# A fused transformer, state-space and routed-expert block on one core: another order of the steps on all five queues, and other PSUM banks

## The chip, the cores and the metric

The kernel runs on one core of one Trainium2 chip. Times are device microseconds (us) of one launch. PE is TensorE, DVE VectorE, ACT ScalarE, POOL GpSimd and SP SyncE, whose queue only issues DMA transfers. The number to predict is the median time of the changed kernel.

## The reference

```
mod = (silu(c) @ wmod).reshape(32, 6, 1, 256)        # sa, ca, ga, sb, cb, gb
h = layernorm(x) * (1 + ca) + sa                      # x: 32 x 512 x 256
# inside block(h):
xn = ln1(h)
attn_out = softmax(causal(q k^T / 4)) v @ o_w + o_b   # 16 heads of 16
x_ssm, z = split(xn @ in_proj_w)                      # 512 channels each
x_c = silu(causal_conv4(x_ssm));  dt = softplus((x_c @ x_proj_w)[:R] @ dt_w + dt_b)
h_t = exp(dt A) h_(t-1) + x_c dt B_t ;  y_t = C_t h_t  # 16 states, 512 tokens
ssm_out = ((y + x_c D) * silu(z)) @ ssm_out_w
x1 = h + alpha attn_out + (1 - alpha) ssm_out
block = x1 + gelu(ln2(x1) @ ffn_w1 + b1) @ ffn_w2 + b2
x = x + ga * block(h)
h = layernorm(x) * (1 + cb) + sb
out = x + gb * (h @ base_w + b + 2 * sum_e softmax(top2(router)) lora_e(h))
```

## The kernel before

The 32 batches are worked off one after the other, in one unrolled stream. All weights stay in SBUF. Each engine has a queue of named steps, and the queue of a batch ("a turn") is a text in the table ORDER: a name with + is that step of the next batch, with - of the batch before, so that about three batches are in work at once. `drive` goes through the text once a batch. The order is thus written out as data. Each step waits for semaphores of the steps that feed it and then issues its instructions; nothing is reordered at run time. A second table, PLACE, gives each step that uses a PSUM bank one of four banks `pM`.

The state-space part is the backbone. It has 64 scans a batch (e = 0 to 63, two of them to a unit k = e/2), each over 128 channels and 512 tokens:

- ACT `decE` writes exp(dt A) to one of two banks `pD`, chosen by e mod 2 (L714).
- POOL `fillK` writes the two inputs of unit k to the ring `state` (L575). It needs the B row of unit k, which SP loads with `rbK` (L430), and room in the ring, which PE's `add` of scan 2k-7 gives.
- DVE `scanE` does the scan (L1207), and `cE` multiplies it by the C row (L1215; SP loads that row with `rcK`). For a quarter of the scans POOL does the multiplication (`pcE`, L563). Until `cE` (or, for those, `scanE`) has read bank `pD`, `dec(E+2)` can't start.
- PE `addE` transposes the product and adds it to `pY` (L945). `gate1` on DVE (L1282) takes the sums when all 64 are in, and PE `skip0` (L936) starts the next sums.

Around it, on the same queues: attention in four head groups (PE `mxG_E` scores, L1033 and L1035, whose maximum DVE takes, L1256; `mtG` turns the maxima and SP sends them back as a matrix row; PE `stG_*` scores again, L1051, ACT exponentials, L813; PE `pvG_*`, L967; DVE `onG` normalises, L1271 and L1273), projections, `sso` (L1073, L1076), the feed-forward part `f1_0` to `f1_7` (L1087), `gelu` (L854), `f2_0` and `f2_1` (PE L1096, DVE L1298), and routing.

ACT `sp2` is the softplus of dt: two instructions on 128 x 1024 elements (L795), with a table load ahead of them and another ahead of the next exponential. The change is in the tables alone; these functions of the kernel are as they were, for instance:

```
elif name == "sp2":
    for jp in range(PASSES):
        dt = dts[:, parity(b), jp * JP:(jp + 1) * JP]
        b.wait(act, dt_x, (jp + 1) * JP)
        act.activation(dt, dt, ACT.Softplus).then_inc(dt_ok.sem, 1)
```

Of the kernel before, what the change touches and what calls it, by code (L numbers as in the profile page):

```python
# [1351 lines left out]

ORDER = {engine: parse(text) for engine, text in {
    "SP": """
        -rc21 -ld3 -rb24 -rc24 -rc23 -rc25 -rb26 -mt2 -rb25 qk3 -rb27 -rc26 -rb29 -rc28 xp -rc27 -rb30 -rb28 -mt3
        ld0 -rb31 rb0 -rc29 -rc30 rc0 l1a rb3 ld2 -rc31 rc1 rc2 rb1 rb4 rb2 rc3 rb5 +load rc4 rb8 rc5 rb6 ld1 -xr
        rc6 rb7 rc8 rc9 rc7 rb9 rb11 rb12 rb13 rc10 rb10 rc11 rc14 rc13 mt0 rc12 rb16 rc15 rb14 rc17 rb15 rc16 rb17
        rb18 rc18 rb19 +qk0 +qk1 +qk2 rc20 rb20 mt1 rc19 x1p rb21 rb22 rc22 rb23 -put
    """,
    "POOL": """  # L1360
        fill7 fill8 +l0s fill9 pc14 pc15 +l0a fill10 +l0b fill11 +l0c fill12 pc22 +l1s fill13 pc23 -x2 -x2b fill14
        -l3s +ql0 fill15 fill16 pc30 -xb +ql1 -route -wkeep fill17 -wnorm pc31 +ql2 fill18 fill19 -gb -put fill20
# [4 lines left out]
        dec5 dec6 z0 dec7 dec8 dec9 dec10 dec11 z1 -l2a dec12 z2 -h2t0 -h2t1 dec13 dec14 dec15 -f1_0 -f1_1 -f1_2
        dec16 -f1_3 dec17 +l0a dec18 -f1_4 -f1_5 dec19 dec20 -f1_6 -f1_7 -gelu dec21 mt0 dec22 z3 dec23 dec24 dec25
        zsilu dec26 +l1a dec27 +xt0 +xt1 st0_0_0 +qk0 dec28 st0_0_1 +qm0 st0_0_2 dec29 +xs0 st0_0_3 st0_1_0 -l3a
        st0_1_1 +qk1 dec30 +qm1 dec31 -h3t0 +xs1 -h3t1 dec32 +qk2 dec33 -route2 st0_1_2 st0_1_3 dec34 mt1 +qm2 -axt  # L1370
        +qk3 dec35 dec36 st0_2_0 -out0 st0_2_2 dec37 -out1 dec38 st0_3_0 st1_0_0 dec39 st1_0_1 st1_0_2 dec40 oe0
        st1_0_3 st1_1_0 st1_1_1 dec41 st1_1_2 st1_1_3 st1_2_0 dec42 dec43 +qm3 st1_2_2 +xs2 +xs3 st1_3_0 dec44 mt2
        dec45 +xsilu dec46 oe1 dec47 +xp st2_0_0 st2_0_1 dec48 st2_0_2 dec49 +dt0 st2_0_3 st2_1_0 dec50 st2_1_1
        dec51 st2_1_2 +dt1 st2_1_3 dec52 mt3 +dt2 st2_2_0 dec53 st2_2_2 dec54 st2_3_0 st3_0_0 st3_0_1 dec55 st3_0_2
        dec56 st3_0_3 dec57 +dt3 oe2 st3_1_0 dec58 dec59 +sp2 dec60 st3_1_1 st3_1_2 st3_1_3 dec61 st3_2_0 st3_2_2
# [3 lines left out]
        mx1_0 mx1_1 add17 add18 add19 -f2_0 -f2_1 mx1_2 +xt0 +xt1 mx1_3 add20 st0_0_0 mx1_4 mx1_5 +qk0 mx1_6 add21
        st0_0_1 +xs0 mx1_7 st0_0_2 mx1_8 add22 st0_0_3 st0_1_0 add23 add24 add25 add26 st0_1_1 +qk1 -h3t0 add27  # L1380
        -h3t1 +xs1 +qk2 -route add28 mx1_9 mx1_10 st0_1_2 add29 st0_1_3 -lora mt1 +qk3 add30 -axt st0_2_0 pv0_0
        -out0 st0_2_2 add31 mx2_0 -out1 mx2_1 st0_3_0 pv0_1 mx2_2 pv0_2 skip1 st1_0_0 pv0_3 mx2_3 mx2_4 add32 add33
        st1_0_1 mx2_5 st1_0_2 mx2_6 add34 mx2_7 mx2_8 st1_0_3 st1_1_0 st1_1_1 mx2_9 pv1_0 add35 st1_1_2 st1_1_3
        add36 st1_2_0 mx2_10 st1_2_2 st1_3_0 +xs2 pv1_1 add37 +xs3 add38 add39 add40 mt2 add41 add42 add43 pv1_2
        mx3_0 mx3_1 pv1_3 on0 mx3_2 +xp mx3_3 mx3_4 add44 st2_0_0 st2_0_1 add45 st2_0_2 mx3_5 +dt0 mx3_6 mx3_7
        st2_0_3 add46 st2_1_0 add47 st2_1_1 mx3_8 st2_1_2 mx3_9 +dt1 st2_1_3 mx3_10 add48 +dt2 mt3 pv2_0 add49
        st2_2_0 st2_2_2 add50 add51 st2_3_0 pv2_1 pv2_2 st3_0_0 st3_0_1 +dt3 st3_0_2 add52 st3_0_3 pv2_3 st3_1_0
        add53 on1 +mx0_0 on2 st3_1_1 add54 +mx0_1 add55 add56 +mx0_2 +v0 add57 +mx0_3 st3_1_2 st3_1_3 add58 pv3_0
        st3_2_0 st3_2_2 pv3_1 st3_3_0 pv3_2 add59 pv3_3 +z0 +v1 on3 add60 add61 +mx0_4 add62 add63 ot0 ot1 +skip0
        yt0 yt1 yt2 +add0 yt3 +add1 +add2 sso0 sso1 +add3 +z1 +add4 +mx0_5 +z2 +add5 +add6 +add7 +add8 +mx0_6 +add9  # L1390
        h2t0 h2t1 +mx0_7 +add10 +add11 +mx0_8 f1_0 f1_1 f1_2 f1_3 f1_4 +mx0_9 f1_5 f1_6 f1_7 +add12 +add13 +add14
        +mx0_10 +add15 +z3 +mt0 +add16
    """,
    "DVE": """
        c13 +l0s scan14 scan15 scan16 c16 scan17 c17 scan18 c18 scan19 mx0_9 c19 mx0_10 scan20 mx1_0 c20 mx1_1
        scan21 c21 scan22 mt0 scan23 +l1s -f2_0 scan24 c24 scan25 c25 scan26 c26 -f2_1 mx1_2 mx1_3 scan27 mx1_4
# [1 line left out]
        mx1_10 c32 +qk2 -esum scan33 -lora mt1 scan34 c33 c34 +qk3 scan35 scan36 c35 mx2_0 c36 gate0 scan37 mx2_1
        scan38 mx2_2 c37 mx2_3 mx2_4 scan39 mx2_5 mx2_6 mx2_7 mx2_8 scan40 mx2_9 scan41 c40 c41 mx2_10 scan42 scan43
        c42 c43 +xs2 +xs3 mt2 scan44 mx3_0 mx3_1 c44 scan45 on0 mx3_2 c45 scan46 mx3_3 scan47 mx3_4 mx3_5 scan48  # L1400
        scan49 mx3_6 mx3_7 c48 c49 mx3_8 scan50 mx3_9 c50 mx3_10 scan51 mt3 c51 scan52 c52 scan53 c53 scan54 scan55
# [55 lines left out]
```

## Time and profile before

| | |
|---|---|
| three runs | 5529.20, 5524.32, 5529.31 us; median 5529.2 |
| the profiled execution | 5525.26 us, span 5523.5 us |
| PE busy | 5113.2 us (93%) |
| DVE busy | 4999.6 us (91%) |
| POOL busy | 4215.9 us (76%) |
| ACT busy | 3967.2 us (72%) |
| mean DMA rate | 147 GB/s |

Busy time is the union of an engine's instructions. In steady state every engine's queue repeats each turn, so one turn can be read for all. PE's ends are modelled, so a full PE is read from its starts: in a stretch where it has no gap, it is the bound.

### The profile page before, as it was taken

What the parts mean: (1) busy time and instruction counts of PE and PEld (TensorE: products, weight loads), DVE (VectorE), ACT (ScalarE), POOL (GpSimd) and SP (SyncE); (2) the same over time, 40 slices, a digit from 0 to 9 for tenths busy, and PEclk for the clock granted to TensorE, in tenths of its full rate; (3) what the DMA queues carried; (4) which work ended last, traced back from release to release, by engine and by line L of the source; (5) the groups of instructions that cost most, each with busy time, mean ns of one, the idle gap of its engine ahead of it and who ended that gap; (6) DMA issues with size and microseconds to landing.
All of it is one profiled execution on the core that took longest, in us unless ns stands there. A gap on an engine that the chain in (4) does not pass through costs nothing.

```text
span 5523.5 us, 94525 instructions
## 1 busy us (share of the span) xinstructions
PE 5113.2 (93%) x32280; PEld 3450.1 (62%) x32280; DVE 4999.6 (91%) x7745; ACT 3967.2 (72%) x6278; POOL 4215.9 (76%) x2641
## 2 busy tenths in 40 slices
...
GB/s 127 140 145 149 153 161 153 146 148 147 155 161 152 142 151 148 156 161 152 142 148 151 154 163 149 143 148 148 153 166 149 142 148 147 155 167 147 144 141 28
DMA packets 521455, 812.22 MB, mean 147 GB/s; under 512 B 80432, under 2 KB 227288, under 8 KB 520976
## 3 DMA queue, kind: packets, MB, share of 16 engines
...
## 4 chain that ended last, share of the span: by engine, by line
PE 44%; DVE 32%; issue 12%; ACT 5%; DMA 3%; POOL 1%; SPq 1%; ACTq 1%; DVEq 0%; POOLq 0%
DVE pD L1207 10%; DVE mx L1256 7%; PE pY L945 7%; PE pM L967 5%; DVE state L1207 4%; PE pM L1076 4%; DVE state L1215 4%; PE pM L1020 3%; DMA bc<-bc_d 3%; PE pM L1051 3%; DVE xc L1247 3%; PE pM L954 2%; PE pM L1002 2%; PE pM L1073 2%; PE pM L1125 2%
## 5 line engine op out<-in xcount | busy, mean ns | idle before, releaser
L575 POOL TENSOR_TENSOR state<-scan_in,bc 128x1024 f32<-128x1024 f32 x1024 | 2412.0, 2365 | 687.1 <-PE pY L945 439.6
L1207 DVE TENSOR_TENSOR_SCAN pD<-pD,state 128x512 f32<-128x512 f32 x1536 | 1849.0, 1217 | 76.3 <-POOL state L575 38.1
L714 ACT ACTIVATE pD<-scan_in,A 128x512 f32<-128x512 f32 x2048 | 1393.6, 688 | 584.0 <-DVE state L1215 482.3
L945 PE MATMUL pY<-ident,state 128*128 128x128 f32 x8192 | 1142.1, 276 | 12.1 <-POOL state L563 7.7
L945 PEld LDWEIGHTS pY<-ident,state 128*128 128x128 f32 x8192 | 912.1, 142 | 260.1 <-issue 172.5
L1215 DVE TENSOR_TENSOR state<-pD,bc 128x512 f32<-128x512 f32 x1536 | 1024.4, 681 | 42.1 <-DMA bc<-bc_d 27.7
L813 ACT ACTIVATE region<-pM 128x512 f32<-128x512 f32 (+1 forms) x1408 | 754.7, 555 | 327.9 <-PE pM L1053 292.5
L1256 DVE TENSOR_REDUCE mx<-pM 128x1 f32<-128x512 f32 (+3 forms) x1408 | 859.7, 630 | 130.0 <-PE pM L1035 127.8
L563 POOL TENSOR_TENSOR state<-state,bc 128x512 f32<-128x512 f32 x512 | 645.5, 1273 | 268.7 <-DVE state L1207 263.5
L1207 DVE TENSOR_TENSOR_SCAN state<-pD,state 128x512 f32<-128x512 f32 x512 | 611.5, 1210 | 78.2 <-ACT pD L714 78.2
L1033 PE MATMUL pM<-region 96*128 96x512 bf16 (+3 forms) x2048 | 527.9, 303 | 120.8 <-DVE mx L1256 73.6
L1051 PE MATMUL pM<-region 98*128 98x512 bf16 (+3 forms) x2048 | 533.1, 302 | 75.0 <-DVE mx L1256 40.4
L1087 PE MATMUL pM<-region,w_f 128*128 128x512 f32 x1024 | 455.3, 598 | 0.9 <-ACT region L845 0.9
L1096 PE MATMUL pM<-w_f,scan_in 128*128 128x256 f32 x2048 | 449.0, 380 | 5.7 <-ACT scan_in L854 5.7
L1096 PEld LDWEIGHTS pM<-w_f,scan_in 128*128 128x128 f32 x2048 | 387.7, 191 | 58.5 <-ACT scan_in L854 6.5
L1033 PEld LDWEIGHTS pM<-region 96*128 96x128 bf16 x2048 | 199.8, 98 | 314.1 <-issue 106.8
L1035 PE MATMUL pM<-mask_qk,identb 128*128 128x128 bf16 x2048 | 394.8, 220 | 0.0
L1053 PE MATMUL pM<-identb,mask_qk 128*128 128x128 bf16 x2048 | 392.2, 220 | 0.0
L967 PE MATMUL pM<-region,vt 128*17 128x512 f32 (+3 forms) x4096 | 369.0, 438 | 0.6 <-ACT region L813 0.6
L1051 PEld LDWEIGHTS pM<-region 98*128 98x128 bf16 x2048 | 199.1, 98 | 266.0 <-ACT region L813 124.0
L1087 PEld LDWEIGHTS pM<-region,w_f 128*128 128x128 f32 x1024 | 190.4, 191 | 218.2 <-issue 208.7
L1247 DVE SCALAR_TENSOR_TENSOR xc<-pM,conv_w,xc 128x511 f32<-128x511 f32 (+2 forms) x384 | 285.6, 744 | 22.1 <-ACT xc L774 13.1
...
## 6 DMA issues: line engine op xcount, KB each, us to landing
...
region<-qk_d SPq DMA_DIRECT2D x256, 64.0 KB, 2.7
...
```

The lines of the kernel that those rows point to most:

```text
L563: nc.gpsimd.tensor_tensor(slot, slot, bc[:, e // JP % BC_SLOTS, 1, :], ALU.mult).then_inc(pp_ok.sem, 1)
L575: nc.gpsimd.tensor_tensor(state[:, at_:at_ + JP], us[:, parity(b), k // N * JP:(k // N + 1) * JP, :], bc[:, k % BC_SLOTS, 0, :].unsqueeze( ...
L714: act.activation(pD[DECAY_BANK[e]][:], dts[:, parity(b), j], ACT.Exp, scale=A[:, j, n:n + 1]).then_inc(a_ok.sem, 1)
L813: act.activation(probs[kb % 2][:, h:h + heads, 0:n], pM[bank_of(name)][:, 0:heads * n].rearrange("p (h t) -> p h t", h=heads), ACT.Exp, sc ...
L945: ins = pe.matmul(y_part(t, e % JP), state[:, e % RING, t * P:(t + 1) * P], ident[:], is_transpose=True, start=False, stop=(e % PASS >= PA ...
L1033: pe.matmul(ps[:, s * n:(s + 1) * n], q[0:QK_ROWS, h, qb * P:(qb + 1) * P], kk[0:QK_ROWS, h, 0:n], start=True, stop=False, skip_group_chec ...
L1051: pe.matmul(ps[:, i * n:(i + 1) * n], kk[0:QK_ROWS + 2, h + i, kb * P:(kb + 1) * P], q[0:QK_ROWS + 2, h + i, kb * P:L], start=True, stop=F ...
L1087: ins = pe.matmul(ps[:], w_f1[:, k, f * P:(f + 1) * P], h2T[:, k], start=(k == 0), stop=(k == KT - 1))
L1096: ins = pe.matmul(ps[:, t * D:(t + 1) * D], gT(b)[:, f, (2 * n + t) * P:(2 * n + t + 1) * P], w_f2[:, f, :], start=(f == 0), stop=(f == FT ...
L1207: v.tensor_tensor_scan(h if e in POOL_C else decay, decay, h, 0.0, ALU.mult, ALU.add)\
L1215: v.tensor_tensor(state[:, e % RING], pD[DECAY_BANK[e]][:], bc[:, slot, 1, :], ALU.mult)\
L1256: v.tensor_reduce(mx[:, g % 2].rearrange("p (h q) -> p h q", q=TB)[:, heads[0]:heads[-1] + 1, qb], pM[bank_of(name)][:, 0:len(heads) * n]. ...
```

## The change

The four texts of ORDER on the compute engines and that of SP are replaced, and the table PLACE with them. Every turn has the same steps with the same instructions as before. The diff of the tables says little to a reader; one pair of lines of it, from DVE's text:

```diff
-        scan56 scan57 c56 c57 on1 scan58 +mx0_0 on2 +mx0_1 scan59 +mx0_2 c58 +mx0_3 c59 scan60 c60 scan61
...
+        scan56 +mx0_0 c56 scan57 +mx0_1 c57 scan58 on2 c58 scan59 +mx0_2 c59 scan60 scan61 c60 c61 +mx0_3 scan62
```

The first place is PE's queue just ahead of the long step `f2_0`, `f2_1` (L1096). Before:

```order
L1020 MATMUL pM<-w_in,xnT 128x512 x2
L1041 MATMUL pM<-ident,mx 16x128
L945 MATMUL pY<-ident,state 128x128 x4
L1033 MATMUL pM<-region 128x512
L1035 MATMUL pM<-mask_qk,identb 128x128
L1033 MATMUL pM<-region 128x512
L1035 MATMUL pM<-mask_qk,identb 128x128
L945 MATMUL pY<-ident,state 128x128 x12
L1096 MATMUL pM<-w_f,scan_in 128x256 x32
```

After:

```order
L1020 MATMUL pM<-w_in,xnT 128x512 x2
L945 MATMUL pY<-ident,state 128x128 x4
L1041 MATMUL pM<-ident,mx 16x128
L1033 MATMUL pM<-region 128x512
L1035 MATMUL pM<-mask_qk,identb 128x128
L1033 MATMUL pM<-region 128x512
L1035 MATMUL pM<-mask_qk,identb 128x128
L945 MATMUL pY<-ident,state 128x128 x12
L1033 MATMUL pM<-region 128x512
L1035 MATMUL pM<-mask_qk,identb 128x128
L1096 MATMUL pM<-w_f,scan_in 128x256 x32
```

Two more `add` steps (of 4 matmuls each; the second one stands further up, behind `f1_7`) and one more `mx` step (`mx1_2`) now stand ahead of `f2_0`; they stood behind `f2_1` or later.

The second place is DVE's queue from the sum of `f2_0` to that of `f2_1` (both L1298). Before:

```order
L1298 TENSOR_TENSOR x<-x,pM 128x512
L1207 SCALAR_TENSOR_TENSOR pD<-pD,state 128x512
L1215 TENSOR_TENSOR state<-pD,bc 128x512
L1207 SCALAR_TENSOR_TENSOR pD<-pD,state 128x512
L1215 TENSOR_TENSOR state<-pD,bc 128x512
L1207 SCALAR_TENSOR_TENSOR pD<-pD,state 128x512
L1215 TENSOR_TENSOR state<-pD,bc 128x512
L1298 TENSOR_TENSOR x<-x,pM 128x512
L1256 TENSOR_REDUCE mx<-pM 128x1 x2
```

After:

```order
L1298 TENSOR_TENSOR x<-x,pM 128x512
L1215 TENSOR_TENSOR state<-pD,bc 128x512
L1207 SCALAR_TENSOR_TENSOR pD<-pD,state 128x512 x2
L1215 TENSOR_TENSOR state<-pD,bc 128x512 x2
L1298 TENSOR_TENSOR x<-x,pM 128x512
L1256 TENSOR_REDUCE mx<-pM 128x1
```

Before, the scans (L1207) between the two sums are 24, 25 and 26; now they are 26 and 27. So `scan27` and `c27`, which stood behind the sum of `f2_1`, stand ahead of it, and one of the two maxima behind it (`mx1_2`) has gone further up. At the start of the same stretch, `c0` and the maximum of `mx0_4` went from behind `gate1` to ahead of it, and `scan1` from ahead to behind.

The third place is DVE's queue beside ACT's softplus. Before, from `scan56` and `scan57` to `c58`:

```order
L1207 SCALAR_TENSOR_TENSOR pD<-pD,state 128x512 x2
L1215 TENSOR_TENSOR state<-pD,bc 128x512 x2
L1271 RECIPROCAL rden<-pM 128x16
L1273 TENSOR_TENSOR region<-pM,rden 128x4x64
L1207 SCALAR_TENSOR_TENSOR pD<-pD,state 128x512
L1256 TENSOR_REDUCE mx<-pM 128x1
L1271 RECIPROCAL rden<-pM 128x16
L1273 TENSOR_TENSOR region<-pM,rden 128x4x64
L1256 TENSOR_REDUCE mx<-pM 128x1
L1207 SCALAR_TENSOR_TENSOR pD<-pD,state 128x512
L1256 TENSOR_REDUCE mx<-pM 128x1
L1215 TENSOR_TENSOR state<-pD,bc 128x512
```

After:

```order
L1256 TENSOR_REDUCE mx<-pM 128x1
L1215 TENSOR_TENSOR state<-pD,bc 128x512
L1207 SCALAR_TENSOR_TENSOR pD<-pD,state 128x512
L1271 RECIPROCAL rden<-pM 128x16
L1273 TENSOR_TENSOR region<-pM,rden 128x4x64
L1215 TENSOR_TENSOR state<-pD,bc 128x512
L1207 SCALAR_TENSOR_TENSOR pD<-pD,state 128x512
L1256 TENSOR_REDUCE mx<-pM 128x1
L1215 TENSOR_TENSOR state<-pD,bc 128x512
L1207 SCALAR_TENSOR_TENSOR pD<-pD,state 128x512 x2
L1215 TENSOR_TENSOR state<-pD,bc 128x512 x2
```

The rows after are `mx0_1 c57 scan58 on2 c58 scan59 mx0_2 c59 scan60 scan61 c60 c61`. Between `c57` and `scan60` there stood `on1`, `scan58`, `mx0_0`, `on2`, `mx0_1`, `scan59`, `mx0_2`, `c58`, `mx0_3` and `c59`. Now `scan58`, `on2`, `c58`, `scan59`, `mx0_2` and `c59` stand there. On ACT `sp2` still stands between `dec59` and `dec60`; the exponential step `st3_1_1` went from behind it to ahead of it. On SP, `rb26` stood ahead of `xp` (the stores of the B and C rows of the next batch, L454 and L456) and now stands behind it.

## Rows read from the trace of the kernel before

**Rows 1.** The page: span, busy time, and the chain that ended last.

```profile
span 5523.5 us, 94525 instructions
PE 5113.2 (93%) x32280; PEld 3450.1 (62%) x32280; DVE 4999.6 (91%) x7745; ACT 3967.2 (72%) x6278; POOL 4215.9 (76%) x2641
PE 44%; DVE 32%; issue 12%; ACT 5%; DMA 3%; POOL 1%; SPq 1%; ACTq 1%; DVEq 0%; POOLq 0%
```

**Rows 2.** Gelu's instruction on ACT: its kind, and first and last start.

```profile
L854 ACT ACTIVATE scan_in<-scan_in x32: 3617/3620/3622, 325.5 to 5464.3; 128x4096 f32<-128x4096 f32 x32
```

**Rows 3.** Busy us and instructions by stretch: PE, PEld, DVE, ACT, POOL; PEclk, DMA, GB/s.

```profile
2708.80:2874.80 166.00, 157.97 (x1011) 106.92 (x1010) 155.75 (x243) 123.72 (x196) 131.60 (x83) 1.00 0.49 151
...
2775.60:2833.80 58.20, 58.19 (x296) 43.62 (x297) 53.48 (x85) 43.98 (x64) 48.44 (x34) 1.00 0.46 139
2833.80:2941.60 107.80, 99.77 (x715) 63.30 (x714) 102.26 (x158) 79.81 (x134) 83.17 (x49) 1.00 0.50 158
```

**Rows 4.** Who PE waited for in 2775.6 to 2833.8: us, times, longest.

```profile
PE pY L936 <- DVE zs L1282: 0.5, 1, 0.5
```

**Rows 5.** Who DVE waited for in 2833.8 to 2941.6, the two largest.

```profile
DVE state L1207 <- ACT pD L714: 2.4, 3, 0.9
DVE mx L1256 <- PE pM L1035: 2.0, 4, 0.7
```

**Rows 6.** Timeline of PE ahead of and in `f2`: start, us, instruction.

```profile
2818.35 0.38 PE L1033 MATMUL pM<-region 96*128 96x512 bf16 x1
...
2818.63 1.48 PE L945 MATMUL pY<-ident,state 128*128 128x128 f32 x12
2819.94 13.98 PE L1096 MATMUL pM<-w_f,scan_in 128*128 128x256 f32 x64
2833.76 0.38 PE L1033 MATMUL pM<-region 96*128 96x512 bf16 x1
```

**Rows 7.** Timeline of DVE beside the softplus, `c56` to `c60`.

```profile
2754.05 1.27 DVE L1215 TENSOR_TENSOR state<-pD,bc 128x512 f32<-128x512 f32 x2
...
2757.57 0.25 DVE L1271 RECIPROCAL rden<-pM 128x16 f32<-128x16 f32 x1
...
2758.20 0.68 DVE L1256 TENSOR_REDUCE mx<-pM 128x1 f32<-128x512 f32 x1
2758.79 1.22 DVE L1207 TENSOR_TENSOR_SCAN pD<-pD,state 128x512 f32<-128x512 f32 x1
2759.93 0.67 DVE L1256 TENSOR_REDUCE mx<-pM 128x1 f32<-128x512 f32 x1
2760.51 0.68 DVE L1215 TENSOR_TENSOR state<-pD,bc 128x512 f32<-128x512 f32 x1
2761.91 0.69 DVE L1256 TENSOR_REDUCE mx<-pM 128x1 f32<-128x512 f32 x1 [0.73 <-PE pM L1035]
2762.52 0.68 DVE L1215 TENSOR_TENSOR state<-pD,bc 128x512 f32<-128x512 f32 x1
2763.12 1.22 DVE L1207 TENSOR_TENSOR_SCAN pD<-pD,state 128x512 f32<-128x512 f32 x1
2764.38 0.69 DVE L1215 TENSOR_TENSOR state<-pD,bc 128x512 f32<-128x512 f32 x1
```

**Rows 8.** Timeline of ACT, `dec58` and `dec59`, the softplus and its two table loads.

```profile
2754.76 1.30 ACT L714 ACTIVATE pD<-scan_in,A 128x512 f32<-128x512 f32 x2 [0.16 <-DVE state L1215]
2756.08 1.28 ACT L795 ACT_TABLE_LOAD   x1
2757.38 2.00 ACT L795 ACTIVATE scan_in<-scan_in 128x1024 f32<-128x1024 f32 x2
2759.40 1.28 ACT L714 ACT_TABLE_LOAD   x1
```

**Rows 9.** Timeline of POOL: `fill28` and `fill29`.

```profile
2746.81 4.68 POOL L575 TENSOR_TENSOR state<-scan_in,bc 128x1024 f32<-128x1024 f32 x2 [5.87 <-DMA bc<-bc_d]
```

**Rows 10.** Timeline of SP: the second store of `xp`, and the row loads behind it.

```profile
2740.72 0.41 SPq L456 DMA_DIRECT2D bc_d<-dbc  x1
2741.17 1.45 SPq L430 DMA_DIRECT2D bc<-bc_d  x3
```

More of the change, by code:

```diff
@@ L1354 @@
     "SP": """
[L1355 to L1358, printed above, removed]
+        -rb24 -rb23 qk2 qk3 +load -ld3 -rc23 -rc25 -rb27 -mt2 -rb25 -rc24 -rc26 xp -rb28 -rb26 -rc27 -rb29 ld0 -rc28
@@ L1365 @@
+        fill31 +u0 +u1 +fill0 pc62 pc63 +fill1 +fill2 +fill3 +fill4 +pc6 +pc7 +fill5 l2s +fill6 +fill7
     """,
     "ACT": """
[L1367 to L1375, printed above, removed]
@@ new lines @@
+        dec36 +qk3 st0_1_3 dec37 -out0 -out1 dec38 st0_2_0 dec39 st0_2_2 st0_3_0 oe0 dec40 +qm3 dec41 st1_0_0
+        st1_0_1 st1_0_2 st1_0_3 st1_1_0 st1_1_1 st1_1_2 st1_1_3 dec42 st1_2_0 st1_2_2 dec43 +xs2 dec44 dec45 +xs3
+        st1_3_0 mt2 +xsilu oe1 dec46 dec47 +xp dec48 st2_0_0 dec49 st2_0_1 st2_0_2 +dt0 st2_0_3 st2_1_0 dec50 dec51
+        st2_1_1 st2_1_2 st2_1_3 st2_2_0 dec52 mt3 st2_2_2 dec53 dec54 +dt1 st2_3_0 dec55 +dt2 dec56 oe2 st3_0_0
+        dec57 st3_0_1 +dt3 st3_0_2 dec58 st3_0_3 st3_1_0 st3_1_1 dec59 +sp2 dec60 st3_1_2 st3_1_3 dec61 st3_2_0
@@ L1377 @@
+        st3_2_2 st3_3_0 dec62 oe3 dec63 +v0 +dec0 +ud +dec1 ot0 ot1 +v1 +dec2 yt0 +dec3 yt1 yt2 yt3 +dec4
     """,
     "PE": """
[L1379 to L1392, printed above, removed]
+        add18 mt0 mx1_0 mx1_1 add19 add20 add21 mx1_2 -f2_0 -f2_1 mx1_3 st0_0_0 add22 +xt0 st0_0_1 add23 +xt1 mx1_4
@@ new lines @@
+        mx3_2 add43 +xp mx3_3 st2_0_0 add44 mx3_4 add45 st2_0_1 add46 st2_0_2 st2_0_3 +dt0 mx3_5 st2_1_0 mx3_6 add47
+        mx3_7 add48 mx3_8 st2_1_1 mx3_9 mx3_10 st2_1_2 st2_1_3 pv2_0 st2_2_0 on1 add49 mt3 st2_2_2 pv2_1 add50 add51
+        +dt1 st2_3_0 +dt2 +dt3 pv2_2 pv2_3 st3_0_0 add52 add53 +mx0_0 st3_0_1 st3_0_2 +mx0_1 st3_0_3 st3_1_0 add54
+        on2 st3_1_1 add55 add56 add57 +v0 +mx0_2 st3_1_2 st3_1_3 st3_2_0 st3_2_2 pv3_0 add58 pv3_1 st3_3_0 pv3_2
+        +mx0_3 pv3_3 add59 add60 +mx0_4 on3 add61 +v1 add62 ot0 ot1 add63 +z0 yt0 +skip0 yt1 yt2 +add0 yt3 +add1
```

62 lines of the change are left out of this document (38 added, 24 removed).

## The prediction

> **What bounds the kernel now.** I read the page first. It shows PE busy 93% and DVE 91%, and the chain that ended last is 44% PE and 32% DVE [rows 1]: two engines share the bound, so the question is which of them is full where. Gelu's instruction gives the length of a turn: 32 of them from 325.5 to 5464.3, so 31 turns of 165.8 us [rows 2], and the stretch that I read is one of 166.0 [rows 3]. Whatever a turn gains or loses counts 31 times.
>
> Then I cut a turn at the two places where the bound changes. Stage 1 goes from PE's `skip0` (2775.6) to the end of PE's `f2_1` (2833.8), 58.2 us. PE is busy 58.19 of it and DVE 53.48 [rows 3]; PE's one wait in it is the 0.5 at its very start [rows 4]. Stage 1 is thus as long as PE's work in it, and DVE has 4.7 us to spare. Stage 2 is the other 107.8 us. DVE is busy 102.26 and idle 5.54, PE is busy 99.77. Of DVE's idle time 2.4 us are waits for the exponentials `dec` and 2.0 for scores from PE [rows 5], so 1.1 are small gaps and lesser waits. Stage 2 is DVE's work plus its waits. ACT (123.7 of 166) and POOL (131.6) have room [rows 3]; they matter only by being late at one place.
>
> **The change, part by part.** No instruction is added or removed, so busy sums of a whole turn hardly move. What can move is how much DVE work lies in the stage where DVE has room, and how long DVE waits in the other.
>
> *Stage 1, PE.* Two more adds and one more `mx` stand ahead of the end of `f2_1`. Twelve add matmuls fill 1.31 us from 2818.63 to 2819.94, so an add (four) costs 0.44; an `mx` takes 0.28, from 2818.35 to 2818.63 [rows 6]. That is 2 x 0.44 + 0.28 = 1.16 us. Stage 1 becomes 58.2 + 1.2 = 59.4 if PE stays without gaps. Its largest risk is `f2_0`, which needs gelu: the `add` steps 12, 13 and 14 now stand between the `f1` steps instead of behind `f1_7`, which puts the last `f1` about 1.3 us (three adds) later, but PE also reaches `f2_0` about 1.2 us later, so I add nothing.
>
> *Stage 1, DVE.* Moved in: `scan1`, `scan27`, `c27` and the maximum of `mx1_2`. Moved out: `c0` and the maximum of `mx0_4`. By the starts of neighbours a scan costs 1.14 (2758.79 to 2759.93), a `c` 0.60 (2762.52 to 2763.12) and a maximum 0.58 [rows 7]; the 384-wide maximum of `mx0_4` I take as 0.5. In: 2 x 1.14 + 0.60 + 0.58 = 3.46. Out: 1.1. The net is 2.4 us more, and 53.5 + 2.4 = 55.9 of 59.4: it fits, with 3.5 us to spare for waits, where before there were 4.7 of them.
>
> *Stage 2, DVE's work.* It loses those 2.4 us: 102.3 - 2.4 = 99.9. A smaller saving comes on top. A `c` right behind its own scan starts 1.26 after it (2763.12 to 2764.38) where another instruction starts after 1.14 [rows 7]. Of such pairs stage 2 had four (52, 53, 60, 61) and now has one (53): 3 x 0.12 = 0.4. DVE's work is then 99.5.
>
> *Stage 2, waits at the softplus.* `dec60` stands behind `sp2` on ACT, and `scan60` waits for it. Counting from the end of `c57`, which frees `dec59`: that end is 2755.32 [rows 7]. `dec59` ends at 2756.06, 0.74 later. Then come load, softplus and load, from 2756.08 to 2760.68, and `dec60` of 0.65 to 0.7 [rows 8]: in all 6.05 us. DVE covers this now with `scan58`, `on2`, `c58`, `scan59`, `mx0_2`, `c59`: 1.14 + 0.63 + 0.60 + 1.14 + 0.58 + 0.60 = 4.7, less 0.1 by which `scan58` starts before `c57` ends, so 4.6 [rows 7]. A wait of 1.5 us is left even if ACT is at `dec59` in time. I take 1.9, since three exponential steps (`st3_0_3`, `st3_1_0`, `st3_1_1`) stand between `dec58` and `dec59` there. Before, the same stretch lasted 7.8 us, from 2755.32 to 2763.12, and held one wait of 0.73 [rows 7]. With 0.4 at `scan61`, the waits for `dec` are 2.3, as large as the 2.4 that they replace. What goes, by my reading of the new order, are the waits at scans 55, 62 and 63: more work now stands between the freeing of their bank and the scan.
>
> At this place a page speaks against the change. The row shows the load starting 0.02 us after `dec59` and the softplus 0.02 after the load, so a switch costs 1.3 [rows 8]. The Trainium skill ("ScalarE: Activation LUTs", section "What ACT_TABLE_LOAD costs") has 1283 ns for the load and 1380 ns of drain with each switch. The trace agrees on the load and shows no drain. By the page two switches would add 2.8 us to the wait, an estimate from its figure.
>
> *Stage 2, other waits.* Of the 2.0 us for scores I keep 1.0: in the order after, PE reaches `mx2_3` behind `pv0_2`, `pv0_3` and their exponentials, so that it is late as before; `mx0_3` has moved behind `c61`, past its lateness of 0.73. Small gaps stay, 1.1. A reading of queues by hand misses waits, above all for banks and transfers: I add 1.1, a quarter of the 4.4 named before. The sum is 2.3 + 1.0 + 1.1 + 1.1 = 5.5, as much as before.
>
> *POOL, SP and the rows.* `fill28` waited 5.87 us for its row and cost DVE nothing [rows 9]. Now `rb26` also stands behind the stores of `xp`; before, the three row loads behind them were issued within 1.9 us of the second store [rows 10]. `scan52` needs `fill26` and comes some 12 us after the exponential pass that frees `xp`, so I cost it at nothing. If that cover is gone, each us of lateness is one us of the turn.
>
> **The sum.** A turn is 59.4 + 99.5 + 5.5 = 164.4 against 166.0, a gain of 1.6 us. Times 31 this is 50 us, and 5525.3 - 50 = 5475. The profiled execution lies 4 us under the median of the runs, so the median becomes 5480, a gain of 0.9%. Start and end of the kernel I leave as they are.
>
> **The rivals.**
>
> *More is gained.* My 1.1 for missed waits isn't there and ACT is prompt at the softplus, 1.5 for 1.9. A turn is then 162.9, and the time 5529 - 3.1 x 31 = 5433. For it: DVE is 94% busy over a turn [rows 3] and most of the waits of before have specific causes. Against it: both engines come closer to full. 0.17.
>
> *Nothing is gained.* Missed waits are 2.7 rather than 1.1; a turn is 166.0 and the time 5529. For it: four shared banks in another order make new collisions that no sum shows. 0.13.
>
> *Slower, by the softplus.* `sp2` stands behind `st3_1_1`, and that needs the maxima of group 3 to go round: DVE's part of `mt3`, a transfer, PE's scores. DVE's `mt3` now stands two steps later, behind `on1` and `scan52`. If this chain is late, ACT stands at an `st3` while `c57` has long ended, and the whole softplus with it, then `scan60` and everything behind it. It decides from a wait of 3.5 us at `scan60` (1.9 + 1.6). At 4.7 a turn is 167.2 and the time 5529 + 37 = 5566. Against it: ACT is idle 28 us of the 107.8 [rows 3]. 0.12.
>
> *Slower, by the row loads.* One row behind `xp` comes 4 us later than DVE can bear: 166.0 + 2.4, so 5603. SP's queue has long waits already, yet DVE felt them little. 0.06.
>
> *Slower, by the drain.* The wait of 4.7 would come without any lateness of ACT, and the time would be 5566 again. The page on ScalarE named above has the rule. The rows show no such gap, so 0.02.
>
> **How the numbers follow.** The forecast keeps 0.50, with a range of its own from 5455 to 5505. A measurement of this kernel can tell about 0.2% (11 us) from no change. Faster: 0.50 + 0.17 = 0.67. Same: 0.13. Slower: 0.12 + 0.06 + 0.02 = 0.20. The range takes in the forecast, "nothing is gained" and half each of the gain of 96 and the loss of 37: 5430 to 5550.
>
> **What would show it.** Right, if stage 1 (from `skip0` to the end of `f2_1`) lasts 59.4 with PE without gaps, DVE is busy 55.9 in it and about 99.5 in stage 2, which lasts 105.0; and if `scan60` waits 1.5 to 2 us for `dec60` while scans 55, 62 and 63 hardly wait. Wrong, if gelu is late for `f2_0`, so that stage 1 gets a gap on PE; if ACT's `dec59` starts more than 2 us behind the end of `c57`; or if the waits for scores double because a bank comes free late.

## The result, and the profile after

The changed kernel takes 5540.55 us (median of 20 runs, 5531.18 to 5551.92), the kernel before 5527.48 (20 runs, 5523.38 to 5536.17). The ratio is 1.0023, with a 95% interval of 1.0017 to 1.0030: the change makes the kernel 0.23% slower, where 0.9% faster was forecast. The profiled execution took 5536.60 us.

Three lines of the page of the kernel after: the span, the busy times, and the chain that ended last by engine.

```profile
span 5534.8 us, 94495 instructions
...
PE 5145.8 (93%) x32280; PEld 3479.3 (63%) x32280; DVE 4992.6 (90%) x7745; ACT 3978.7 (72%) x6278; POOL 4207.4 (76%) x2641
...
PE 82%; ACT 7%; DVE 6%; issue 3%; POOL 1%; DMA 1%; ACTq 1%; SPq 0%; POOLq 0%; DVEq 0%
```

Against [rows 1], DVE lost 7 us of work and PE gained 33, although no matmul was added. The chain, which was divided between PE and DVE, now runs over PE. That alone says nothing of the cause, since PE has 81% of the chain in the faster kernel a_gaps below as well. But an engine that needs more time for the same instructions is the first sign of what happened.

The second sign is in the lengths of the turns. From one `gate1` to the next, 24 turns of the kernel after last 167.3 us each, and two last 164.1, next to each other in the middle of the run. I forecast 164.4. So the forecast turn exists, and it is rare. Here are both kinds, as windows of the kernel after (columns: stretch, length, then busy us and count of PE, PEld, DVE, ACT and POOL, the granted clock of TensorE as a share of 2.4 GHz, the DMA share and GB/s). First a whole turn of each kind, then stage 1 and stage 2 of each, cut as in the prediction.

```profile
2277.40:2441.50 164.10, 156.47 (x1009) 106.97 (x1008) 155.42 (x242) 124.11 (x197) 131.35 (x83) 1.00 0.52 153
2774.30:2941.60 167.30, 159.62 (x1009) 108.26 (x1009) 155.54 (x241) 124.11 (x197) 131.29 (x83) 0.98 0.52 150
...
2279.33:2338.23 58.90, 58.90 (x304) 44.15 (x303) 55.79 (x88) 44.92 (x65) 50.20 (x35) 1.00 0.50 143
2338.23:2443.41 105.18, 97.55 (x707) 62.82 (x706) 99.61 (x154) 79.17 (x133) 81.13 (x49) 1.00 0.53 160
2608.99:2667.88 58.89, 58.89 (x304) 44.14 (x303) 55.79 (x88) 44.91 (x65) 50.17 (x35) 1.00 0.45 142
2667.88:2776.27 108.39, 100.62 (x708) 64.11 (x706) 99.73 (x154) 79.17 (x133) 81.13 (x49) 0.97 0.53 155
```

Read downwards: DVE, ACT and POOL do the same work in the same time in both kinds of turn, and stage 1 is the same. Stage 2 is 3.2 us longer, PE is busy 3.1 us longer in it, and its granted clock is 0.97 instead of 1.00. DVE, whose work plus waits is the length of stage 2, waits those 3.2 us for PE's scores (us in total, times, longest; first in the stage 2 of 105.18, then in that of 108.39):

```profile
DVE mx L1256 <- PE pM L1035: 2.5, 4, 1.4
DVE mx L1256 <- PE pM L1035: 5.7, 6, 2.9
```

The record of the clock shows why: in a turn of 167.3, TensorE is granted 0.50, which is 1.2 GHz, in two stretches of 3.4 us. Between 280 and 5350 us the kernel after has 51 such low stretches and the kernel before has 3. Two of them, and what PE did ahead of the first one:

```profile
2591.40:2594.80 3.40, 0.44 (x4) 0.16 (x3) 1.75 (x4) 3.37 (x5) 3.34 (x2) 1.00 1.01 292
2596.40:2599.40 3.00, 3.00 (x18) 1.04 (x15) 1.75 (x3) 1.09 (x2) 2.04 (x1) 0.50 0.99 236
...
2726.10:2729.40 3.30, 3.30 (x8) 1.71 (x6) 3.26 (x7) 2.00 (x3) 0.56 (x1) 0.50 0.53 198
```

**The first low stretch** stands behind a gap of PE. It is in the turn from 2441.5 to 2607.0, which has this low stretch alone and lasts 165.6. The timeline of ACT shows the softplus block of that turn: `dec59`, load, softplus, load, `dec60`, and then the exponentials of `st3_1_2` and `st3_1_3`.

```profile
2588.33 0.69 ACT L714 ACTIVATE pD<-scan_in,A 128x512 f32<-128x512 f32 x1
2589.03 1.28 ACT L795 ACT_TABLE_LOAD   x1
2590.33 2.00 ACT L795 ACTIVATE scan_in<-scan_in 128x1024 f32<-128x1024 f32 x2
2592.35 1.28 ACT L714 ACT_TABLE_LOAD   x1
2593.65 0.69 ACT L714 ACTIVATE pD<-scan_in,A 128x512 f32<-128x512 f32 x1
2594.27 0.85 ACT L813 ACTIVATE region<-pM 128x384 f32<-128x384 f32 x2
```

In the new PLACE, `st3_2_0` writes the bank of `st3_1_2`, whose exponential stands behind `sp2`. PE therefore has nothing to do for 2.96 us. The timeline of PE in a turn without low stretches and in the turn of the rows above (the last matmul of `st3_1_3`, then `st3_2_0`, `pv3_0`, `add58`, `pv3_1`):

```profile
2427.55 0.22 PE L1053 MATMUL pM<-identb,mask_qk 128*128 128x128 bf16 x1
2430.72 0.28 PE L1051 MATMUL pM<-region 98*128 98x256 bf16 x1 [2.96 <-ACT region L813]
...
2431.55 1.05 PE L967 MATMUL pM<-region,vt 128*17 128x512 f32 x8
2432.53 0.66 PE L945 MATMUL pY<-ident,state 128*128 128x128 f32 x4
2433.12 0.84 PE L967 MATMUL pM<-region,vt 128*17 128x384 f32 x8
...
2591.62 0.22 PE L1053 MATMUL pM<-identb,mask_qk 128*128 128x128 bf16 x1
2594.80 0.28 PE L1051 MATMUL pM<-region 98*128 98x256 bf16 x1 [2.96 <-ACT region L813]
...
2595.62 1.23 PE L967 MATMUL pM<-region,vt 128*17 128x512 f32 x8
2596.78 1.12 PE L945 MATMUL pY<-ident,state 128*128 128x128 f32 x4
2597.82 1.48 PE L967 MATMUL pM<-region,vt 128*17 128x384 f32 x8
```

The gap is the same in both. Behind it, the same `add58` takes 0.66 us in the one turn and 1.12 in the other, and `pv3_1` 0.84 and 1.48. DVE stands behind them: it waits for the scores of `mx0_3`, and the wait doubles (DVE's timeline: the first row below is `scan60` with its wait for `dec60`, the second `mx0_3` in the turn without low stretches, the third `mx0_3` in the turn with them).

```profile
2594.37 2.60 DVE L1207 TENSOR_TENSOR_SCAN pD<-pD,state 128x512 f32<-128x512 f32 x2 [1.65 <-ACT pD L714]
...
2435.50 0.69 DVE L1256 TENSOR_REDUCE mx<-pM 128x1 f32<-128x512 f32 x1 [1.43 <-PE pM L1035]
...
2601.08 0.69 DVE L1256 TENSOR_REDUCE mx<-pM 128x1 f32<-128x512 f32 x1 [2.94 <-PE pM L1035]
```

**The second low stretch** falls on `xp` (L1009), which takes 5.11 us instead of 3.60. PE had short waits ahead of it, the last two at `mx3_1` and `mx3_2` (PE's timeline, the turn without low stretches first):

```profile
2394.93 0.39 PE L1033 MATMUL pM<-region 96*128 96x512 bf16 x1 [0.64 <-DVE mrow L1263]
...
2395.90 0.39 PE L1033 MATMUL pM<-region 96*128 96x512 bf16 x1 [0.52 <-ACT region L831]
...
2396.63 3.60 PE L1009 MATMUL pM<-xc,w_xp 128*128 128x512 f32 x8
...
2724.58 0.39 PE L1033 MATMUL pM<-region 96*128 96x512 bf16 x1 [0.96 <-DVE mrow L1263]
...
2725.55 0.39 PE L1033 MATMUL pM<-region 96*128 96x512 bf16 x1 [0.53 <-ACT region L831]
...
2726.46 5.11 PE L1009 MATMUL pM<-xc,w_xp 128*128 128x512 f32 x8
```

These waits don't differ between the kinds of turn: in each of the 30 turns, PE's waits from `mx3_0` to `xp` add up to 1.3 to 1.5 us, with a low stretch behind them or without. What differs is the turn before. Each of the 24 turns with a low stretch at `xp` follows a turn that had one behind the gap ahead of `st3_2_0`.

**The account.** Of the 31 turns the last one ends with the drain of the program, so I take 30. In the profiled executions these 30 last 4981.3 us before and 5006.9 after, 25.6 more. The time up to the first `gate1` is 7.6 us shorter after, the last turn 4.8 and the rest behind it 2.0. 25.6 - 7.6 - 4.8 - 2.0 = 11.2, which is the 11.3 us between the two profiled executions. Against 30 turns of 164.1, the kernel after loses 83.9 us to the longer ones. At 164.1 throughout it would take 5536.6 - 83.9 = 5453 us, somewhat better than the forecast. The 20 executions agree with this reading: the mean granted clock is 0.972 in the fastest of them (5531.18) and 0.967 in the slowest (5551.92), and between them the time rises as the clock falls. The experiments ask whether the low stretches are what costs these 84 us, and whether PE's gaps are what brings them.

### The profile page after: what moved, and what is told of

Its sections match the earlier page's. It is cut to its first block, busy times and chain, and to the rows that moved or that the text cites. A ratio compares the mean times of both kernels' runs of the same rounds, so it can differ in the third digit from the quotient of the medians.

```text
span 5534.8 us, 94495 instructions
## 1 busy us (share of the span) xinstructions
PE 5145.8 (93%) x32280; PEld 3479.3 (63%) x32280; DVE 4992.6 (90%) x7745; ACT 3978.7 (72%) x6278; POOL 4207.4 (76%) x2641
## 4 chain that ended last, share of the span: by engine, by line
PE 82%; ACT 7%; DVE 6%; issue 3%; POOL 1%; DMA 1%; ACTq 1%; SPq 0%; POOLq 0%; DVEq 0%
PE pY L945 14%; PE pM L1096 8%; PE pM L1087 8%; PE pM L967 6%; PE pM L1051 5%; PE pM L954 4%; PE pM L1002 4%; PE pM L1033 4%; PE pM L1076 4%; PE pM L987 4%; PE pM L1020 4%; PE pM L1009 3%; DVE mx L1256 2%; PE pM L1125 2%; PE pM L1073 2%
## 5 line engine op out<-in xcount | busy, mean ns | idle before, releaser
L1207 DVE TENSOR_TENSOR_SCAN pD<-pD,state 128x512 f32<-128x512 f32 x1536 | 1849.8, 1218 | 63.7 <-ACT pD L714 56.8
L945 PE MATMUL pY<-ident,state 128*128 128x128 f32 x8192 | 1196.9, 279 | 15.3 <-DVE state L1215 9.5
L945 PEld LDWEIGHTS pY<-ident,state 128*128 128x128 f32 x8192 | 930.3, 143 | 355.2 <-issue 258.5
L813 ACT ACTIVATE region<-pM 128x512 f32<-128x512 f32 (+1 forms) x1408 | 740.3, 556 | 333.2 <-PE pM L1053 238.6
L1207 DVE TENSOR_TENSOR_SCAN state<-pD,state 128x512 f32<-128x512 f32 x512 | 604.8, 1206 | 26.1 <-ACT pD L714 26.0
L1033 PE MATMUL pM<-region 96*128 96x512 bf16 (+3 forms) x2048 | 541.2, 303 | 75.0 <-DVE mrow L1263 25.7
L1096 PE MATMUL pM<-w_f,scan_in 128*128 128x256 f32 x2048 | 450.6, 381 | 5.7 <-ACT scan_in L854 5.7
L1096 PEld LDWEIGHTS pM<-w_f,scan_in 128*128 128x128 f32 x2048 | 388.2, 191 | 61.4 <-ACT scan_in L854 6.5
L967 PE MATMUL pM<-region,vt 128*17 128x512 f32 (+3 forms) x4096 | 387.0, 468 | 1.9 <-ACT region L813 0.3
```

The source lines that it names most:

```text
L813: act.activation(probs[kb % 2][:, h:h + heads, 0:n], pM[bank_of(name)][:, 0:heads * n].rearrange("p (h t) -> p h t", h=heads), ACT.Exp, sc ...
L945: ins = pe.matmul(y_part(t, e % JP), state[:, e % RING, t * P:(t + 1) * P], ident[:], is_transpose=True, start=False, stop=(e % PASS >= PA ...
L967: ins = pe.matmul(pO[32 * h:32 * h + HD + 1, kb * P:L], vt[:, kb, g * G + h, :], probs[kb % 2][:, h, 0:L - kb * P], start=(kb == 0), stop= ...
L1033: pe.matmul(ps[:, s * n:(s + 1) * n], q[0:QK_ROWS, h, qb * P:(qb + 1) * P], kk[0:QK_ROWS, h, 0:n], start=True, stop=False, skip_group_chec ...
L1096: ins = pe.matmul(ps[:, t * D:(t + 1) * D], gT(b)[:, f, (2 * n + t) * P:(2 * n + t + 1) * P], w_f2[:, f, :], start=(f == 0), stop=(f == FT ...
L1207: v.tensor_tensor_scan(h if e in POOL_C else decay, decay, h, 0.0, ALU.mult, ALU.add)\
```

## The experiments

The theory (T1): the new order opens gaps on PE; behind them TensorE is granted 1.2 GHz for a while; that costs 1.6 us for each stretch, and without it the turn is 164.1. The rival (T2): the low stretches are a by-product, and the turn is longer because of waits that the sum missed. Each ratio below is to the kernel before on the same chip.

### Filling the gaps of PE

The filler is a repetition of matmuls that the step issues anyway, into the same bank, with the same values; the last pair leaves what one pair would have left. In a gap of PE it uses idle time alone.

```diff
-                    for s, h in enumerate(heads):
+                    for s, h in list(enumerate(heads)) * (1 + FILL.get(name, 0)):
...
-                    for i in range(HEADS[kb]):
+                    for i in list(range(HEADS[kb])) * (1 + FILL.get(name, 0)):
...
+FILL = {'st3_1_3': 9}                               # a_gap_a
+FILL = {'mx3_0': 3, 'mx3_1': 2}                     # a_gap_b
+FILL = {'st3_1_3': 9, 'mx3_0': 3, 'mx3_1': 2}       # a_gaps, and b_gaps on the kernel before
+FILL = {'st3_1_3': 4}                               # a_gap4
+FILL = {'st0_0_3': 9}                               # a_busy
```

**a_gap_a**, the gap ahead of `st3_2_0` alone:

> The changed order with one edit: PE repeats the score matmuls of st3_1_3 nine times more into the same bank (same result, about 2.0 us a turn), where PE otherwise stands still for 3.0 us behind the softplus (gap A). Theory 1 (clock): the two stretches of about 3.4 us a turn in which TensorE is granted 1.2 GHz follow PE's gaps, and each costs 1.6 us. The one behind gap A goes; turns of 167.3 become about 165.7 or less, mean clock 0.98 or more, time about 5495. Theory 2 (order): the turn is 167.3 because of the waits of the new order itself, and the clock is a bystander. More PE work gives 5540 or more.

**a_gap_b**, the waits ahead of `xp` alone:

> The changed order with repeats in the other place where PE has gaps, ahead of xp (gap B): mx3_0 three times more and mx3_1 twice more, 1.4 us a turn. Theory 1: the low stretch that falls on xp goes, xp lasts 3.5 instead of 5.1 us; time about 5495. Theory 2: 5540 or more, since mx3_0 and mx3_1 come later.

**a_gaps**, both:

> The changed order with both sets of repeats. Theory 1: no low stretch in the steady turns, clock back at 0.985, turns of 164.1 as in the three turns that had none, time about 5445 to 5455, which beats both kernels. Theory 2: 5540 or more.

**b_gaps**, both in the kernel before:

> Control: the kernel before with the same repeats in the same three steps (st3_1_3 nine times, mx3_0 three, mx3_1 two more). Its steady turns have no low stretch, so by the clock theory there is nothing to win: 5528 or more, up to 5528 + 31 x 1.0 = 5560 where the repeats hold up ACT or DVE. If repeats of matmuls helped for any other reason (keeping weights or banks warm), this kernel would become faster too, 5500 or less.

**a_busy**, nine more pairs in the kernel after where PE has no gap:

> The changed order with the same nine repeats (2.0 us a turn) in st0_0_3, where PE has no gap and its work goes on. Clock theory, in which the place counts: both low stretches stay, the repeats cost up to 2.0 us a turn, 5540 to 5600. If only the total of PE work in a turn mattered, the time would fall to about 5465 as with the repeats in gap A.

**a_gap4**, four more pairs in place of nine:

> The changed kernel with the pair of matmuls of st3_1_3 issued five times in all, which fills some 0.9 us of the 2.96 us gap instead of 2.0 us. If the low stretch behind the gap depends on the gap's length, it goes wholly (about 5465, as with 2.0 us), in part of the turns (5470 to 5530), or not at all (5540). If the gain of the longer fill came from something other than the clock, the time should fall in proportion to the fill: about 5505.

Measured (the gap ahead of `st3_2_0` and the low stretches are of the profiled execution; the stretches are counted between 280 and 5350 us):

| kernel | median us | ratio (95% interval) | most frequent turns | gap | low stretches |
|---|---|---|---|---|---|
| after | 5540.55 | 1.0023 (1.0017 to 1.0030) | 167.3 | 2.96 | 51 |
| a_gap_a | 5463.72 | 0.9883 (0.9869 to 0.9896) | 164.1 | 0.95 | 6 |
| a_gap_b | 5500.25 | 0.9951 (0.9939 to 0.9964) | 165.5, 165.6 | 2.96 | 27 |
| a_gaps | 5461.08 | 0.9880 (0.9865 to 0.9895) | 164.1 | 0.95 | 2 |
| a_gap4 | 5513.07 | 0.9982 (0.9973 to 0.9990) | 167.3 and 164.1 | 2.06 | 37 |
| a_busy | 5604.37 | 1.0137 (1.0122 to 1.0153) | 168.1, 169.8 | 2.96 | 43 |
| b_gaps | 5615.52 | 1.0157 (1.0143 to 1.0171) | 168.7 | none | 1 |

More matmuls made the kernel 79 us faster. T2 can't say why, and T1 forecasts it, if with a time somewhat too low (5445 to 5455). One turn in the middle of a_gaps, as a window, and PE's row behind the shortened gap of an earlier turn:

```profile
2738.10:2902.20 164.10, 159.77 (x1037) 109.10 (x1036) 155.42 (x242) 124.14 (x197) 131.35 (x83) 1.00 0.51 153
...
2398.51 0.28 PE L1051 MATMUL pM<-region 98*128 98x256 bf16 x1 [0.95 <-ACT region L813]
```

PE has 28 more matmuls in it than in the turns of the kernel after, is busy as long as in the turns of 167.3, and the turn lasts 164.1 with a clock of 1.00. With `xp`'s place filled alone (a_gap_b) the low stretch there is gone, the one behind the gap ahead of `st3_2_0` stays in most turns, and the turn is 165.5, half-way between.

Filler costs time where PE has no gap. b_gaps is 1.6% slower than the kernel before, 2.7 us a turn for matmuls that keep PE busy 3.3 us (159.77 less 156.47, in a_gaps). That is more than the 1.0 a turn that I had expected at most (5560 us against 5615 measured). a_busy stays at 1.4% over with its low stretches still there, one in its turns of 168.1 and two in those of 169.8; less 1.6 for each, both are 166.5 or 166.6, so that the filler costs 2.4 to 2.5. So it isn't the added matmuls that hold the clock up; it is their place.

The Trainium skill ("TensorE: Matmul & The Clock Gate", section "A second HAM failure mode: psum-queue depth-cycling") tells of a kernel in which PE cycles through PSUM banks and has short idle times between groups of matmuls, and in which the clock swings between its two levels for that reason. The runs agree that such idle time can do it: here it was one gap of 2.96 us behind a shared bank, on an engine that is 93% busy.

a_gap4 shows that the gap alone doesn't decide. Two turns of it as windows, and the start of `st3_2_0` in each:

```profile
2435.90:2600.00 164.10, 157.35 (x1018) 107.56 (x1017) 155.43 (x242) 124.19 (x197) 131.51 (x83) 1.00 0.51 153
2765.50:2932.80 167.30, 160.52 (x1018) 108.83 (x1017) 155.54 (x242) 124.17 (x197) 131.42 (x83) 0.98 0.50 150
...
2587.22 0.28 PE L1051 MATMUL pM<-region 98*128 98x256 bf16 x1 [2.06 <-ACT region L813]
...
2918.60 0.28 PE L1051 MATMUL pM<-region 98*128 98x256 bf16 x1 [2.06 <-ACT region L813]
```

With the same gap of 2.06 us, ten turns last 164.1 and sixteen last 167.3 or 167.4. They come in rows, with a turn of 165.6 on the way to the long ones. The median of 5513 alone doesn't decide, since it is only 8 us from the 5505 of a gain in proportion to the filler. The turns do: they are a mixture of two kinds, and the filler of 0.9 us made the long kind less frequent. Nor are the two low stretches independent. In a_gap_a only the first gap was filled, and I had expected the stretch at `xp` to stay (5495). It was left in 4 of 30 turns, behind the same waits of 1.3 to 1.5 us, and the time was 5464. So the waits ahead of `xp` are needed for a low stretch there, since a_gap_b has none, but by themselves they seldom bring one. What picks the kind of a turn isn't settled by these runs.

### Taking the cause of the gap away, and making it longer

The gap ahead of `st3_2_0` is there because ACT is in the softplus block. So I shortened and lengthened the block, in both orders. a_exp and b_exp leave out the logarithm of the softplus and with it the two table loads.

```diff
-                        act.activation(dt, dt, ACT.Softplus).then_inc(dt_ok.sem, 1)
+                        act.activation(dt, dt, ACT.Exp).then_inc(dt_ok.sem, 1)     # a_exp, b_exp
...
                         act.activation(dt, dt, ACT.Softplus).then_inc(dt_ok.sem, 1)
+                        if jp == 0:
+                            act.activation(side[:], eps4[:, 0:1], ACT.Gelu)        # a_long, b_long
```

**a_exp**:

> The changed order with Exp in place of Softplus (leaves out the logarithm, so dt is wrong): no table loads around it, the block on ACT is 2.6 us shorter. Theory 1: PE's gap A shrinks from 3.0 to about 0.5 us, its low stretch goes, and scan60 doesn't wait: one dip less (1.6) and 1.3 to 1.6 us less waiting, so a turn of about 164.2 with the dip at B or 162.6 without, time 5440 or less. Theory 2 (waits alone): a turn loses the 1.65 us at scan60 and no more, 165.6, time about 5490.

**b_exp**:

> The kernel before with Exp in place of Softplus (leaves out the logarithm): the block on ACT is 2.6 us shorter. In this order dec60 waited for c58 and not for ACT, so I expect little: waits at scans 60 to 63 change by under 0.5 us a turn, 5510 to 5530. If the order of before were as exposed to the block as the changed one (which lost 2.6 us a turn with Exp), it would be 5450.

**a_long**:

> The changed kernel with the same extra Gelu. The softplus block bounds a wait there already (Exp in its place gave 0.973), so all 2.9 us should be exposed: 5540 + 31 x 2.9 = 5630. The two low stretches of TensorE are there already, so the clock theory adds nothing or one more of them, 5630 to 5680. A theory in which the new order hides the softplus says 5540.

**b_long**:

> The kernel before with one more Gelu, on a tile of 128x1, after the first softplus half: two more table loads stand inside the softplus block, which grows by some 2.9 us a turn; the output is unchanged. In the order of before the 2.0 us softplus left the time alone (Exp in its place gave a ratio of 1.000), so there is slack of a size not yet known. If the 2.9 us are hidden like the 2 x 1.7 us that Exp saved: 5530. If they come out behind the exponentials as waits of DVE: up to 31 x 2.9 = 90 us, 5620. If the gap that opens on TensorE before st3_2_0 also brings a stretch at 1.2 GHz each turn, at 1.6 us: 5620 to 5670, with the granted clock down from 0.985 to about 0.975.

| kernel | median us | ratio (95% interval) | turns | low stretches |
|---|---|---|---|---|
| a_exp | 5380.79 | 0.9733 (0.9720 to 0.9747) | 161.5 | 10 |
| b_exp | 5529.28 | 1.0001 (0.9992 to 1.0010) | 166.0 | 1 |
| a_long | 5626.70 | 1.0188 (1.0174 to 1.0202) | 168.4 to 171.1 | 40, most of 6.8 us |
| b_long | 5576.55 | 1.0097 (1.0083 to 1.0110) | 167.0 to 167.8 | 4 |

The timeline of ACT in a_long has the longer block, and PE's shows what it does to the gap (line numbers are 1 to 3 higher there):

```profile
2640.18 1.28 ACT L798 ACT_TABLE_LOAD   x1
2641.48 0.20 ACT L798 ACTIVATE side<-eps 128x1 f32<-128x1 f32 x1
2641.68 1.28 ACT L796 ACT_TABLE_LOAD   x1
...
2646.50 0.40 PE L1054 MATMUL pM<-region 98*128 98x256 bf16 x1 [5.88 <-ACT region L816]
```

2.9 us of ACT become 2.9 us of PE's gap (2.96 to 5.88), and the time grows by 1.9% less 0.2%, some 90 us, which is 31 x 2.9. Both kernels have low stretches, so this match needs a check. In turns of a_long of 168.4, 169.4 and 170.8 PE is busy 157.84, 158.84 and 160.13 us, which is 1.4, 2.4 and 3.7 more than in a turn at the full clock (156.47). Less that, each is 167.0 or 167.1, and 164.1 + 2.9 is 167.0. In the new order every us of the block is on the path. In the order of before it isn't: the shorter block gave nothing, and the longer one cost 53 us, 1.7 a turn, so that 1.2 us of it were hidden. (The shorter block took 2.6 us from ACT's work in a turn, 123.7 to 121.1, and not the "2 x 1.7" that my expectation for b_long names.) b_long opens no gap over 1.6 us on PE and has 4 low stretches; my bound of 5620 to 5670 for a clock that falls there didn't come into play.

a_exp is the other way to close the gap, without filler: it shrinks to 0.36 us, the low stretches go from 51 to 10, and the turn loses 5.8 us. 3.2 of these are the clock's (167.3 to 164.1), and of the other 2.6, 1.65 are `scan60`'s wait, which is gone, and 0.6 are part of that of `mx0_3`.

### Undoing places 1 and 2

Here I took a_gaps, so that the clock is out of the question, and put back the order of before around `f2` on PE and on DVE. That should cost what the prediction says it saves.

```diff
-        add18 mt0 mx1_0 mx1_1 add19 add20 add21 mx1_2 -f2_0 -f2_1 mx1_3 st0_0_0 add22
+        add18 mt0 mx1_0 mx1_1 add19 -f2_0 -f2_1 add20 add21 mx1_2 mx1_3 st0_0_0 add22
...
-        mx1_1 mx1_2 scan22 scan23 scan24 c24 mt0 scan25 +l1s -f2_0 c25 scan26 scan27 c26 c27 -f2_1 mx1_3 scan28
+        mx1_1 scan22 scan23 scan24 c24 mt0 scan25 +l1s -f2_0 c25 scan26 c26 -f2_1 mx1_2 mx1_3 scan27 c27 scan28
```

(`mx1_2` also gets another bank, as its place needs.) In a_undo2, ACT's `st0_0_0` stands ahead of `dec29` as well:

```diff
-        zsilu dec26 dec27 +l1a dec28 dec29 st0_0_0 +xt0
+        zsilu dec26 dec27 +l1a dec28 st0_0_0 dec29 +xt0
```

**a_undo**:

> The changed order with both sets of repeats, and places 1 and 2 undone: add20, add21 and mx1_2 stand behind f2_1 on PE, mx1_2, scan27 and c27 behind f2_1 on DVE (bank of mx1_2: 2). By my sum stage 1 becomes 1.2 us shorter and stage 2 gets 2.3 us of DVE work back: a turn of 164.1 + 1.1 = 165.2, time 5461 + 34 = 5495. Rival: stage 2 had slack in its waits and takes the work in, then the turn shortens to 163 to 164 and the time is 5461 or less.

**a_undo2**:

> The partly undone order (places 1 and 2 as before, with both fills) and st0_0_0's exponential ahead of dec29 on ScalarE, so that it no longer waits behind DVE's c27. If the terms of stage 1 and stage 2 add up as the prediction had them, the turn is 165.2 us and the time about 5495. If the 2.35 us wait of TensorE before xt1 has another cause than ScalarE's queue, the time stays at about 5590.

a_undo took 5594.84 us, ratio 1.0119 (1.0105 to 1.0133), and turns of 167.8 or some 169.4: 100 us more than expected. The trace shows a new wait of PE, 2.35 us ahead of `xt1`: its bank is held until the exponential of `st0_0_0`, which stands behind `dec29` on ACT, which waits for DVE's `c27`, and that is what I had moved back. A step moved on one queue was late on two others. Behind this gap, too, the clock fell: 13 of the 30 turns have a low stretch there, at 66 to 68 us of the turn, which the kernel after never has. The row of PE behind the gap:

```profile
2534.96 0.63 PE L954 MATMUL pM<-ident,ht 128*128 128x128 f32 x4 [2.35 <-ACT region L813]
```

a_undo2 removes that chain: 5559.46 us, 1.0069 (1.0055 to 1.0082), turns of 167.3 with a full clock. It is still 3.2 us a turn over a_gaps, where my sum had 1.1. Stages 1 and 2 of a_gaps as windows, then those of a_undo2:

```profile
2575.95:2634.84 58.89, 58.89 (x304) 44.11 (x303) 55.78 (x88) 44.91 (x65) 50.17 (x35) 1.00 0.47 142
2634.84:2740.03 105.19, 100.91 (x736) 65.02 (x734) 99.60 (x154) 79.19 (x133) 81.17 (x49) 1.00 0.54 160
```

```profile
2622.90:2681.52 58.62, 57.95 (x295) 43.18 (x294) 53.50 (x85) 44.55 (x64) 47.96 (x34) 1.00 0.45 141
2681.52:2790.22 108.70, 102.23 (x746) 65.88 (x744) 102.07 (x157) 79.35 (x133) 83.43 (x49) 1.00 0.49 155
```

DVE's waits for scores in stage 2, in a_gaps and then in a_undo2 (us in total, times, longest):

```profile
DVE mx L1256 <- PE pM L1035: 2.5, 4, 1.4
DVE mx L1256 <- PE pM L1035: 3.6, 6, 1.4
```

DVE's work in a_undo2 is 2.28 us less in stage 1 and 2.47 more in stage 2, which is the 2.4 of the prediction. PE's work in stage 1 is 0.94 less, for which I had 1.16. The rest of the 3.2 is waits: PE's 0.67 for gelu at `f2_0`, and DVE's idle time in stage 2, which rose from 5.59 to 6.63: the rows show it as waits for PE's scores, 1.1 us more. DVE also waits 2.0 us at `scan22` and 1.7 at `f2_1`, but in stage 1, where PE is the bound. So the terms of the work held, and an order that is patched in one place brings new waits with it: in the order of before, which was made as a whole, stage 2 has 5.54 us of them [rows 3].

## Why the prediction was wrong

**What held.** Stage 1 lasts 58.9 us with PE without gaps (forecast 59.4), DVE is busy 55.79 in it (55.9). Stage 2 has 99.61 us of DVE's work (99.5) and lasts 105.18 in a turn at the full clock (105.0), so waits and small gaps are 5.57 (5.5). The turn is 164.1, forecast 164.4. That the 5.5 came out is in part luck, as said below under what was mis-sized. `scan60` waits 1.65 (1.9, within 1.5 to 2), and the waits at scans 55, 62 and 63 are gone. Gelu isn't late for `f2_0`, and no load of a row is late. The softplus block ran as [rows 8] had it, with 0.02 us between its parts, so the drain that the Trainium skill puts there ("ScalarE: Activation LUTs", section "What ACT_TABLE_LOAD costs") doesn't show after the change either.

**What failed.** It is the step "Stage 2 is DVE's work plus its waits", with PE's gaps in stage 2 costed at nothing. I checked PE for one thing, whether it would be late for DVE, and let all its instructions keep their durations from a trace in which the clock was full. The runs showed a price for idle time on an engine that isn't the bound: behind a gap of 2.96 us come 1.6 us of slower matmuls that DVE waits for, and in most turns the same once more at `xp`. Two stretches a turn took 3.2 us where the change had gained 1.9. None of my rivals named the clock. One of my signs of being wrong came true, though: the waits for scores more than doubled, from 2.0 us in stage 2 before to 5.7 in the long turns, in part behind a bank that comes free late. Of those 5.7, 3.2 are the clock's.

**The step that should have led there** is one I took half-way. I followed `sp2` to `dec60` and `scan60` and saw DVE's wait. I didn't follow it to the exponentials behind `dec60`, the bank that they free and PE's next step. That wait is longer than DVE's, 2.96 against 1.65. Before, no wait of PE in the steady turns was over 1.6 us.

**What was mis-sized.** The waits of DVE for scores: I kept 1.0 us and had `mx0_3` "past its lateness". In a turn at the full clock they are 2.5 us in stage 2, 1.43 of them at `mx0_3`, since PE comes late from its gap. My allowance of 1.1 for missed waits, and the 0.4 at `scan61` which isn't there, covered this by luck. The start and the end of the kernel, which I left as they were, became 14.4 us shorter (7.6, 4.8 and 2.0), so that the loss looks smaller than it is in the steady turns (25.6 us). The two adds and the `mx` ahead of `f2_1` cost 0.94 for my 1.16. The outer range, 5430 to 5550, was said to take in half of the gain of 96; its lower end is the whole of it (5529 - 96 = 5433).

**The rival on the other side**, slower by the softplus, named the right instruction and the wrong victim: `dec59` wasn't late, and `scan60` didn't wait over 3.5 us.
